# A four-layer vision tower on one core: products of a token tile moved into the norm, and some GpSimd work moved to VectorE and ScalarE

## What is computed

```python
x  = tokens(img)                              # norm, projection, norm, position table
x  = L0_attn(x); x = L0_ffn(x)                # 16 heads, two score terms; 16 experts, 4 per token
x  = L1_attn(x); x = L1_ffn(x)                # 2 heads with rotation; 8 experts of width 352, 2 per token
x  = L2_attn(x); x = L2_ffn(x)                # 16 heads; then latent attention ("mla"), a shared and 7 routed experts
x  = L3_attn(x); x = L3_ffn(x)                # attention over the 16 images; 8 experts that take 148 tokens each
# every part begins with a norm of x, and every attention or router begins with products of the normed x:
v      = norm(x) @ Wv + bv                    # values
logits = norm(x) @ Wr                         # router
latent = rmsnorm(x) @ W_lat                   # the two latents of mla
```

## Time and profile before

| | us |
|---|---|
| median of 3 runs | 851.51 (849.39 to 854.37) |
| the profiled execution | 857.64 |
| its span, first to last instruction | 855.5 |
| PE busy | 742.4 (87%) |
| DVE, ACT, POOL busy | 393.4, 221.2, 333.6 |
| mean granted TensorE clock | 0.932 |

### The profile page before, as it was taken

How to read it: one execution, slowest core, us unless ns; L and a number is a source line. 1 busy time by engine, 2 the same in 40 slices (tenths; PEclk the granted TensorE clock), 3 DMA queues, 4 the chain that set the end, 5 groups by cost and what they waited for, 6 DMA issues and landing times. The chain is left out here.

```text
span 855.5 us, 16310 instructions
## 1 busy us (share of the span) xinstructions
PE 742.4 (87%) x5946; PEld 657.4 (77%) x5946; DVE 393.4 (46%) x1093; ACT 221.2 (26%) x588; POOL 333.6 (39%) x399
## 2 busy tenths in 40 slices
PE   6897898799999788899997897798999878879997
PEld 4785688688888677899986686577888754779996
DVE  3745967545433465411132864475431337532211
ACT  1021410254445032123201410142234025111120
POOL 2336541456664131244323423521354278243211
PEclk9897997899999999799998898798999988989999
DMA  9303005588885750787524101200486630255603
GB/s 366 162 7 49 8 2 176 182 246 236 241 239 160 246 178 1 265 269 233 180 76 98 13 2 38 22 3 31 113 270 191 271 52 11 69 198 215 233 17 101
DMA packets 79203, 116.94 MB, mean 137 GB/s; under 512 B 44566, under 2 KB 58071, under 8 KB 77207
## 3 DMA queue, kind: packets, MB, share of 16 engines
q1 hardware_dynamic: 66741, 88.46, 33.4%
q0 software_dynamic: 7968, 20.20, 7.9%
q10 hardware_dynamic: 4418, 7.25, 2.3%
HBM read 99.29 MB, written 16.60 MB: 135 GB/s over the span
## 5 line engine op out<-in xcount | busy, mean ns | idle before, releaser
L280 PE MATMUL ps<-const_sb 128*128 128x128 f32 x910 | 131.3, 303 | 0.0
L280 PEld LDWEIGHTS ps<-const_sb 128*128 128x128 f32 x910 | 124.6, 218 | 1.3 <-issue 0.5
L1840 PE MATMUL ps<-l0e_xg_fm,l0e_ring 128*128 128x128 f32 x544 | 72.7, 277 | 6.8 <-ACT l0e_up_sb L1924 3.1
L1840 PEld LDWEIGHTS ps<-l0e_xg_fm,l0e_ring 128*128 128x128 f32 x544 | 67.6, 191 | 12.8 <-issue 7.5
L922 PE MATMUL ps<-x_fm,w_sb 128*128 128x296 f32 x208 | 54.3, 413 | 0.0
L308 POOL TENSOR_TENSOR norm_r<-norm_ve,const_sb 128x2 f32<-128x2 f32 (+1 forms) x27 | 19.5, 724 | 88.3 <-DVE norm_ve L301 64.0
L1840 PE MATMUL ps<-l1e_xg_fm,l1e_ring 128*128 128x128 f32 (+1 forms) x408 | 50.8, 275 | 1.1 <-ACT l1e_xg_fm L1901 0.6
L1840 PEld LDWEIGHTS ps<-l1e_xg_fm,l1e_ring 128*128 128x128 f32 (+1 forms) x408 | 48.2, 182 | 2.5 <-issue 1.7
L1741 POOL DMA_INDIRECT l0e_y_scratch<-l0e_y_tm,l0e_rows_u x34 | 35.9, 1057 | 33.9 <-ACT l0e_y_tm L1948 29.9
L922 PEld LDWEIGHTS ps<-x_fm,w_sb 128*128 128x128 f32 x208 | 39.4, 190 | 11.8 <-DVE l1p_rot_b L953 0.3
L1726 POOL DMA_INDIRECT l0e_xg_tm<-x_scratch,l0e_rows_u x34 | 33.3, 980 | 22.1 <-PE ps L1804 9.3
(11 more groups left out here) (496 smaller groups left out, 1585.2 us busy)
## 6 DMA issues: line engine op xcount, KB each, us to landing
l0e_ring<-in_l_experts SPq DMA_DIRECT2D x34, 514.0 KB
l1e_ring<-in_l_experts SPq DMA_DIRECT2D x17, 704.0 KB
l2e_ring<-in_l_experts SPq DMA_DIRECT2D x16, 512.0 KB
expert_w<-in_l_experts SPq DMA_DIRECT2D x4, 2048.0 KB
l_more_w<-in_l_experts SPq DMA_DIRECT2D x4, 2048.0 KB
l0e_down_w<-in_l_experts SPq DMA_DIRECT2D x1, 4096.0 KB, 15.9
l1e_down_w<-in_l_experts SPq DMA_DIRECT2D x1, 3072.0 KB, 11.8
w_sb<-in_weights SPq DMA_DIRECT2D x2, 1032.0 KB, 6.8
```

The lines of the kernel that those rows point to most:

```text
L280: pe.matmul(ps[:, bank, 0:P], ident, ident, start=True, stop=True)
L1840: mm = pe.matmul(ps[0:widths[m], which, m * P:(m + 1) * P], w_n[:, c:c + widths[m]], x_n[:, k, :], start=(k == 0), stop=(k == KT - 1))
```

## The change

The norm's transposes of tile t now write one PSUM bank, ACT alone copies both halves of a tile to `x_fm` as soon as it is turned (one instruction, or two where a scale is applied), and PE follows each tile at once with its products: `follow` is the values of the coming attention in four norms (tokens, and the ends of the expert stages of layers 0, 1 and 2), the logits of the coming router in four, the latents in one. The dummy products inside the norm are gone. The blocks behind lose those products; DVE finds the values of all tiles in PSUM at the start.

Beside it: the token block's order on PE and DVE is changed; keys of the first two pairs of `attend` are shared between POOL and DVE (one image each), and in `attend_across` POOL and DVE make two key blocks each for the first group; the last unit's rotation sum is DVE's; in the routers of layers 0 and 1 half of the marks goes to ACT; `prepare` of the latent attention moves from the latents' block into the projection's.

```diff
+        def values_of(layer, terms):
+            def follow(pe, t):
+                if t == 0:
+                    pe.wait_ge(loaded[layer], 16)
+                for k, (w, x) in enumerate(terms):
+                    pe.matmul(ps[:, 4 + t // 2, (t % 2) * D:(t % 2 + 1) * D], x[:, t * P:(t + 1) * P], w,
+                              start=(k == 0), stop=(k == len(terms) - 1))
+            return follow
+        def logits_of(router):
+            width = router.shape[2]
+            def follow(pe, t):
+                for k in range(KT):
+                    pe.matmul(ps[:, 7, t * width:(t + 1) * width], x_fm[:, k, t * P:(t + 1) * P], router[:, k, :],
+                              start=(k == 0), stop=(k == KT - 1))
+            return follow
+        def latents_of(w):
+            def follow(pe, t):
...
+                    pe.matmul(ps[:, 4 + t // 4, (t % 4) * P:(t % 4 + 1) * P], w[:, k, :], x_fm[:, k, t * P:(t + 1) * P],
+                              start=(k == 0), stop=(k == KT - 1))
-        def norm_parts(src, dst, rms=False, scale=None):
+        def norm_parts(src, dst, rms=False, scale=None, follow=None):
...
-                for part, (c0, c1) in enumerate(((0, 512), (512, PADDED))):
-                    dve.wait_ge(norm["turned"], 2 * n + part + 1)
-                    o, i = x_fm[:, 1, c0:c1], ps[:, 2 + part, 0:c1 - c0]
...
             def tensor(pe):
+                def turn(t):
+                    pe.wait_ge(norm["normed"], TILES * n + t + 1)
+                    if t == 4:
+                        pe.wait_ge(norm["copied"], TILES * n + 1)
+                    for k in range(KT):
+                        mm = pe.transpose(ps[:, t % 4, k * P:(k + 1) * P], dst[:, t, k * P:(k + 1) * P], ident)
+                    mm.then_inc(norm["turned"], 1)
+                def go_on(t):
+                    pe.wait_ge(norm["copied"], TILES * n + t + 1)
+                    follow(pe, t)
+                turn(0)
+                turn(1)
+                go_on(0)
+                go_on(1)
+                turn(2)
+                turn(3)
+                go_on(2)
+                turn(4)
+                go_on(3)
+                go_on(4)
+            def scalar(act):
                 for t in range(TILES):
-                    if t in (2, 4):
-                        stay_awake(pe, 3)
...
-                stay_awake(pe, 3, 4)
+                    act.wait_ge(norm["turned"], TILES * n + t + 1)
...
+                        act.activation(x_fm[:, :, c], ps[:, t % 4, 0:KT * P].rearrange("p (k r) -> p k r", k=KT), ACT.Copy)\
+                            .then_inc(norm["copied"], 1)
```

The token block:

```diff
                         pe.wait_ge(loaded["ident"], 16)
+                        stay_awake(pe, 6, 2)
...
                         offsets_of(0)
+                        turn_coefs(1)
                         products(3)
-                        turn_coefs(1)
-                        products(4)
                         offsets_of(1)
                         turn_coefs(2)
+                        products(4)
                         offsets_of(2)
-                        stay_awake(pe, 14)
+                        stay_awake(pe, 8)
...
                         def ready(dve, g):
-                            if g + 1 < len(GROUPS):
-                                first(g + 1)
+                            if g == 1:
+                                first(1)
+                                first(2)
```

Attention, projection, latents and routers:

```diff
+                SHARED = 2
...
-                                for s in range(2):
...
+                                for s in range(1 if n < SHARED else 2):
+                                    keys(pool, n, m, s).then_inc(s_kbd, 1)
...
+                        for n in range(SHARED):
+                            for m in range(NMM):
+                                keys(dve, n, m, 1).then_inc(s_kbd_v, 1)
...
-                        for t in range(TILES):
+                        for t in range(0 if made else TILES):
...
+                            if made:
+                                src = ps[:, 4 + t // 2, (t % 2) * D:(t % 2 + 1) * D]
...
+                                if i == len(units) - 1:
+                                    dve.wait_ge(s_t, i + 1)
+                                    dve.wait_ge(s_free[slot], i // slots + 1)
+                                    dve.tensor_tensor(dst[:, c0:c0 + HALF], t1[:, i % RING, :], t2[:, i % RING, :],
+                                                      ALU.add).then_inc(s_sum, 1)
...
-                            for i, ((_, _, dst, _, _, _), half) in enumerate(units):
+                            for i, ((_, _, dst, _, _, _), half) in enumerate(units[:-1]):
...
-            ON_POOL = 3
+            ON_POOL, AT_FIRST = 3, 2
...
-        def latents(tag, lat, terms, prepare):
+        def latents(tag, lat):
...
+                        act.activation(lat[:, 0:512], ps[:, 4, 0:512], ACT.Copy).then_inc(s_cp, 1)
...
+                        dve.tensor_copy(lat[:, 512:TOKENS], ps[:, 5, 0:TOKENS - 512]).then_inc(s_cp, 1)
...
-                        prepare(pool)
...
-                        for c, what in enumerate((tokens_4, slots_4)):
-                            pool.tensor_tensor(marks_5[:, :, :, c, :], in_4, what, ALU.mult).then_inc(s_marks, 1)
+                        pool.tensor_tensor(marks_5[:, :, :, 0, :], in_4, tokens_4, ALU.mult).then_inc(s_marks, 1)
+                        if dense is not None:
+                            pool.tensor_tensor(marks_5[:, :, :, 1, :], in_4, slots_4, ALU.mult).then_inc(s_marks, 1)
...
+                            act.wait_ge(s_in, 1)
+                            for i in range(top):
+                                act.activation(marks[:, i * TILES:(i + 1) * TILES, 1, :],
+                                               in_tile[:, i * TILES:(i + 1) * TILES, :], ACT.Copy, scale=float(i + 1))\
+                                    .then_inc(s_marks, 1)
```

More of the change, by code:

```diff
@@ L267, in build @@
         loaded = {n: sem(f"loaded_{n}") for n in [*WEIGHTS, "cols", "tok_rows", "rows", "ident", "consts"]}
-        norm = {n: sem(f"norm_{n}") for n in ("chain", "var", "rstd", "normed", "turned", "copied_a", "copied_v")}
+        norm = {n: sem(f"norm_{n}") for n in ("chain", "var", "rstd", "normed", "turned", "copied")}
         stat_bufs = {n: (sb(f"{n}_stats", [P, TILES, 2, 6]), sb(f"{n}_mv", [P, TILES, 2]), sb(f"{n}_ve", [P, TILES]),
@@ L871, in _, with project @@
                                                          [PAIR, HEADS, HD], o=1), ALU.mult).then_inc(s_ctx, 1)
-        def project(tag, layer, jobs, v_terms, v_bias=None, v_tm=None, pads=(), between=None, prepare=None, then=None, layers=()):
+        def project(tag, layer, jobs, v_terms, v_bias=None, v_tm=None, pads=(), between=None, prepare=None, then=None, layers=(), made=True):
             rot = jobs[0][1] is not None
@@ L1401, in step @@
                                 pool.wait_ge(s_scores, n - 1)
-                            for c in range(ON_POOL):
+                            for c in range(AT_FIRST if isinstance(n, int) and n == 0 else ON_POOL):
                                 block_diagonal(pool, n, u, c).then_inc(s_kbd, 1)
@@ L1575, in tiled_experts @@
         def tiled_experts(tag, w_in, E, top, widths, router, bias=None, clipped=False, down_b=None,
-                          dense=None, source=None, then=None):
+                          dense=None, source=None, then=None, after=None):
             NT = (TOKENS * top + E * (P - 1)) // P
@@ L1661, in tiled_experts @@
                 s_back = [sem(f"{tag}_back{t}", st) for t in range(TILES)]
-                vector, gpsimd, tensor, scalar = norm_parts(h, xn)
+                vector, gpsimd, tensor, scalar = norm_parts(h, xn, follow=values_of(after, value_terms(f"{after}_v")))
                 RW = router.shape[2]
@@ L2283, in _ @@
                     def _(pe):
-                        router = weight("l3_router")
-                        for t in range(TILES):
-                            for k in range(KT):
-                                mm = pe.matmul(ps[:, 0, t * E:(t + 1) * E], x_fm[:, k, t * P:(t + 1) * P],
-                                               router[:, k, :], start=(k == 0), stop=(k == KT - 1))
-                        mm.then_inc(s_mm, 1)
                         stay_awake(pe, 12)
@@ L2605, in build @@
             placed = placed_values("mlaa", st)
-            wl = weight("mla_lat")
-            latents("mlal", lat, [(wl[:, k, :], x_fm[:, k, :]) for k in range(KT)], placed[3])
+            latents("mlal", lat)
             one = {n: weight(f"mla_{n}", 1)[:, 0, :] for n in ("q", "qrot", "k_lat", "v")}
```

120 lines of the change are left out of this document (43 added, 77 removed).

## The result

The changed kernel took 843.84 us in the median of 8 runs (838.53 to 848.2); the kernel before, beside it, 852.03. The ratio is 0.9899, with a 95% interval of 0.9855 to 0.9944: faster, but by 8 and not by 21. Repeated on other chips the ratio was 0.9891 and 0.9882. The measured 843.84 lies above the forecast of 830.5 and above the upper end, 841, of the prediction's range.

What follows compares the result with a forecast made beforehand. PE is busy 87%, but the change was priced by the seams between stages: ten terms sum to 21.0 us, taking the profiled 857.64 to 836.6 and the median 851.51 to 830.5; range 821 to 841.

Steps and rivals of the forecast that it cites:

- that is 0.3 later ... Sum 7.8: Four routers: logits computed in the norm, its end 0.3 later at 2.4 GHz in layer 3's; 7.8 us saved in all.
- the marks: Routers of layers 0 and 1: marks split between POOL and ACT, listing sooner; 1.3 and 0.4 us saved.
- all at 1.2: Lower bound of the logits' saving, with all four routers' norms at 1.2 GHz: 5.7 us.
- Against: the first expert tiles wait for ACT's copy, not for a weight.: Routers' first expert tiles: the argument against late expert weights, a case costing 9.5 us.
- rival 3: Routers: expert weights are late, so 7.8 and 1.7 are lost at the first expert tile; 840 us, chance 0.06.
- So it ends 2.6 sooner: Layer 2's projection: SP's block ends 2.6 us sooner as DVE's adds shrink; with the norm's loss, 0.5 taken.
- The attentions: Attention blocks: keys shared between POOL and DVE save 0.1 in layer 0, 0.5 in layer 2, 0.4 in layer 3.
- Values of layers 0 and 1: Norms and projections of layers 0 and 1: values computed in the norm save 2.0 and 1.9 us.
- The latents: Latents' block: products in the norm and POOL's clearing moved out save 2.6 us (2.0 to 3.3).
- The token block: Start of layer 0: DVE no longer idles for the second group, first norm starts 1.5 us sooner (0.8 to 2.0).
- rival 2: All norms: the real products raise the clock, 28.8 us saved; 823 us, chance 0.14.
- rival 1: Norms: the clock is at 1.2 GHz in most, 12.3 us saved; 839 us, chance 0.18.

Runs made afterwards that it cites:

- ahead: Changed kernel with dummies back in the four routers' norms, only ahead of the first turn, as many as idle time holds: 821.81 us, ratio 0.9851.
- both_back: Changed kernel with values and logits back in their blocks, norms without dummies: 836.84 us, ratio 1.0056.
- rest: both_back with three dummies each put back in three places of the eight norms concerned: 835.85 us, ratio 1.0004.
- ahead_lists: Changed kernel with the dummies of ahead and other engines' lists shortened in the projections of layers 1 to 3: 816.75 us, ratio 0.9798.
- values_back: Changed kernel with the values of the four layers back in their projections: 831.62 us, ratio 0.9976.
- keys_back: Changed kernel with the keys as before, all of the first pairs' on POOL: 827.89 us, ratio 0.9916.
- last: ahead_lists with layer 0's keys as before the change, all on POOL there: 817.27 us, ratio 0.9748.
- before_again: The kernel before, unchanged, in a second profiled execution: 836.24 us, ratio 1.0008.
- combined: ahead_lists with half of layer 1's down weights issued later, the sigmoid's table loaded earlier and layer 0's keys as before: 826.1 us, ratio 0.9898.
- awake: Changed kernel with dummies back in the four routers' norms, 12 to 34 ahead of the first turn, two each in three places behind: 827.87 us, ratio 0.9919.

## Why the prediction was wrong

The direction and most of the mechanisms were right, the size was not: 8 for 21. The steps, as the prediction put them:

- **Logits, "that is 0.3 later ... Sum 7.8".** This failed first, and it is the largest part. The sum of 7.8 is 4 x 2.2 less 1.0, so I let the four norms' ends move by 1.0 in all; I looked for which clock each norm had before instead of what the dummies did for it. The tails grew by 1.1, 1.1, 2.2 and 1.8, 6.1 in all, at 1.2 GHz nearly throughout. With the marks the four routers gave 4.6 where I had 9.5. The bound that I gave for "all at 1.2" (5.7) was too mild as well: it left out that the dummies in the router's own block would run long. ahead shows 4 to 5 to be the clock.
- **"Against: the first expert tiles wait for ACT's copy, not for a weight."** That dismissed rival 3, and it holds for the start of before, not for one that comes 2 sooner. In layer 1 the gathered rows then take 1.2 to 1.4 longer, beside the weights' transfer, the stage gains nothing, and with a longer tail in front the whole 2.6 is lost. For the other routers rival 3 is wrong. In the latent attention's, PE's dense products hold the counting (6.1 in the block, the choice ready at 4.5), but they held it before too (9.2, 7.0 and 9.2), and the stage is 3.0 shorter: what is lost there is the tail. Layer 0's gave 4.1 for 2.9: its first tile is at 21.2 in the block and was at 25.3.
- **Layer 2's values, "So it ends 2.6 sooner".** It ended 0.2 sooner, 14.3 long where I had written 10 to 12. I counted DVE's adds and SP's issues, not the landing between: the weights issued first set when SP may go on. This was in the trace of before, as SP's start 7.9 into a block whose adds ended 5.1 into it. The norm ahead grew by 1.8 where I had 1.2.
- **The attentions.** Forecast -1.0 for layers 0 to 3 together, measured +3.9: 1.7 in layer 0, 1.7 in layer 1, 0.5 in layer 2. In layer 1 nothing of the attention was edited. In the third profile of each kernel it is

```profile
301.40:316.30 14.90, 14.37 (x182) 13.37 (x182) 6.57 (x13) 5.83 (x15) 0.00 (x0) 0.81 0.17 41
```

after, and before

```profile
311.90:324.30 12.40, 11.85 (x182) 11.08 (x182) 6.57 (x13) 5.50 (x15) 0.00 (x0) 1.00 0.01 1
```

with the same 182 instructions on PE and a clock of 0.81 and 1.00. Layer 1's attention took 12.4 in all three profiles of before, none of it at 1.2 GHz, and 12.4, 14.8 and 14.9 after, the longer two with over 5 us at 1.2. Of the 14 other kernels' traces 11 have 3.4 us or more at 1.2 GHz there; both_back, rest and ahead_lists have none. That the clock fell is shown; why it does so is not: the length of the projection ahead doesn't decide it, for it fell in values_back, whose projection is 17.9 long, and not in ahead_lists, whose projection is 11.9. In layer 0, keys_back and last had 41.9 and 42.5, which speaks for the shared keys; that block also varied from 41.5 to 44.7 with the time at 1.2 GHz (6.8 to 17.1). Compared at the same time at 1.2 GHz, shared keys cost nothing at 6.8 us of it (41.5 and 41.9, where before_again has 41.9), 0.6 at 10.2 (means of three and of four traces) and 1.5 at 13.7 (the mean of seven against combined alone), so both seem to have a part, and their sizes stay open.
- **Right.** Values of layers 0 and 1 (-2.0 and -2.3 for -2.0 and -1.9). The latents, 3.4 for 2.6: the block is 0.88 long, with ACT's copy of 512 in 0.60 as forecast. The token block, 2.6 for 1.5. In layer 3 the projection is 2.7 shorter, as forecast, and ends by POOL, 10.5 into the block that starts at 671.27 (the tail ahead of it took 2.3 of that back, where I had 1.2 to 2.5):

```profile
673.53 6.93 POOL L1378 MEMSET l3a_v_bd<- 128x8192 f32 x1
...
680.42 1.31 POOL L1379 COPY l3a_v_bd<-const_sb 128x640 f32<-128x640 f32 x1
```

- **Rivals 1 and 2 were both true, of different norms.** Each rival had one clock for all nine. The values' norms stayed at or came to full rate, as rival 2 said; the logits' norms mostly fell to half, as rival 1 said. Neither rival's time, 839 and 823, came out. The Trainium skill, "TensorE: Matmul & The Clock Gate", What's actually happening, has it that activity releases the rate; the trace agrees for the norms with values, while the row of 722.30 has PE busy for 6.56 of 6.80 and 0.58 all the same.

And one step of method failed: I took the sum against one execution of before, at a clock of 0.932. It was no typical one, and the range should have held what differs between executions: the runs of before on the first chip alone span 14 us (847.14 to 861.24).

## What to carry to other kernels

When filler is taken out and real work put in its place, ask which clock it will run at, and look for a row with such work: here four norms fell to 1.2 GHz in most traces, and a few dummies in a wait ahead of them, fewer than the wait holds, kept two of them up and gave about 5 us back. When a block's head is cut, follow the critical chain past the cut to the next two arrivals (a landing transfer, a filler, another product in the same list): in layer 1's router and layer 2's projection there was one within 1 to 3 us. Where executions differ by more than an edit is worth, compare several profiles block by block, and don't trust a pair that agrees with the forecast.

## What was not expected of the hardware

- A write of 128 KB took 5.2 us to land when 1032 KB had been issued just ahead of it, and 1.8 when that was issued last. The Trainium skill, "DMA: Bandwidth & Descriptors", Two DMAs through the same engine are not ordered, says that within one queue of one DMA engine descriptors start in order; both rows are in line with it.
- 1 us more at 1.2 GHz went with 0.32 us of span in the mean of 112 runs of the kernel before, not with 0.5. Taking it away is worth nothing where the dummies cost as much: awake had 31 us less of it than the changed kernel and was no faster.
- The granted clock fell in layer 1's attention in two of three executions of one kernel and in none of three of the other, with the same 182 PE instructions in that block.
